# A six-block decoder on one core: stage order re-sought with a plan that counts changes of the matmul tile shape, and the top rows of the second attention turned in one transposition

## What is computed

```python
x = layernorm(x + attention0(x))      # 32 heads; low-rank q and kv, rope, causal softmax, 128 wide values
x = layernorm(x + adjacency(ctx, x))  # top-k mask of ctx Q K^T (64 wide), symmetrised
x = layernorm(x + experts(x))         # 7 routed experts (top 2) and a shared one, 256 wide
x = layernorm(x + attention1(x))      # 16 heads of 16, rope, causal softmax; see below
x = layernorm(x + bilinear(x, ctx))   # kv = ctx W_k; softmax(layernorm((x kv) kv^T))
x = layernorm(x + ffn(x))             # silu(x Wg) * (x Wu), 1024 wide, then down

# attention1
q, k = rot(q), rot(k)
scores = einsum('bthd,bshd->bhts', q, k / 4)
attn = softmax(scores + causal_mask)
ctx = einsum('bhts,bshd->bthd', attn, v)
```

## Time and profile before

| | |
|---|---|
| median of 3 runs | 703.93 us (702.81 to 706.13) |
| span of the profiled execution | 700.4 us |
| busy PE | 680.6 us (97%), 4886 matmuls |
| busy DVE, ACT, POOL | 531.1 us (76%), 494.1 us (71%), 394.8 us (56%) |
| chain that ended last | PE 77%, POOL 9%, DVE 8%, issue 3% |

### The profile page before, as it was taken

How to read it: one execution, slowest core, us unless ns; L and a number is a source line. 1 busy time by engine, 2 the same in 40 slices (tenths; PEclk the granted TensorE clock), 3 DMA queues, 4 the chain that set the end, 5 groups by cost and what they waited for, 6 DMA issues and landing times.

```text
span 700.4 us, 14717 instructions
## 1 busy us (share of the span) xinstructions
PE 680.6 (97%) x4886; PEld 574.7 (82%) x4886; DVE 531.1 (76%) x1677; ACT 494.1 (71%) x1276; POOL 394.8 (56%) x657
## 2 busy tenths in 40 slices
PE   8899999999999999999998999999989999999995
PEld 6578998888888888888886888898977787678885
DVE  2678989888697869878889776565689777866537
ACT  3789774888659784788879786646766686857631
POOL 4659732885267741698867655544791322435625
PEclk9999999999999999999999999999999999999999
DMA  8671001240341401122012002111120000101201
GB/s 293 167 229 42 17 1 40 53 122 2 109 133 32 122 1 54 46 54 61 2 49 89 1 28 63 47 46 46 46 91 3 5 2 4 48 1 46 91 1 60
DMA packets 34418, 41.06 MB, mean 59 GB/s; under 512 B 6620, under 2 KB 27238, under 8 KB 34344
## 3 DMA queue, kind: packets, MB, share of 16 engines
q1 hardware_dynamic: 33800, 39.80, 19.4%
q10 hardware_dynamic: 544, 0.33, 0.2%
HBM read 30.02 MB, written 1.05 MB: 44 GB/s over the span
## 4 chain that ended last, share of the span: by engine, by line
PE 77%; POOL 9%; DVE 8%; issue 3%; DMA 1%; SPq 1%; ACT 0%; POOLq 0%; DVEq 0%
PE bank L1184 68%; PE bank L1198 8%; POOL stat L2341 3%; POOL qT L2341 1%; PE bank L1455 1%; POOL probs L2338 1%; DMA qT<-xT_plain 1%; DVE top_tok L2238 1%; POOL probs L2341 1%; POOL w_split_lo L2341 1%; DVE g_pair_lo L1896 1%; SPq L2622 1%; DVE y L1899 1%; POOL stat L2338 1%; DVE bn L1911 1%
## 5 line engine op out<-in xcount | busy, mean ns | idle before, releaser
L2338 POOL TENSOR_SCALAR probs<-probs,soft 128x256 f32<-128x256 f32 (+1 forms) x256 | 104.5, 429 | 48.4 <-DVE soft L2031 46.7
L1686 ACT ACTIVATE probs<-probs,soft 128x256 f32<-128x256 f32 (+1 forms) x256 | 113.0, 447 | 13.5 <-DVE soft L2023 12.9
L1184 PE MATMUL bank<-xT_hi,w_split_hi 128*128 128x512 f32 x256 | 103.7, 405 | 3.5 <-POOL w_split_lo L2341 3.2
L2341 POOL TENSOR_TENSOR w_split_lo<-w_raw,w_split_hi 128x512 fp32r<-128x512 f32 (+2 forms) x57 | 72.3, 1275 | 55.1 <-ACT w_split_hi L1592 54.9
L1184 PE MATMUL bank<-xT_lo,w_split_hi 128*128 128x512 f32 x256 | 101.0, 394 | 0.0
L1184 PE MATMUL bank<-keyT,qT 128*128 128x256 f32 (+1 forms) x512 | 93.4, 330 | 0.5 <-POOL qT L2341 0.3
L2023 DVE CUSTOM_DVE_ANT_0 probs<-bank,mask 128x256 f32<-128x256 f32 (+1 forms) x256 | 78.9, 353 | 19.8 <-PE bank L1184 19.1
L1184 PEld LDWEIGHTS bank<-keyT,qT 128*128 128x128 f32 x512 | 81.8, 190 | 12.3 <-issue 2.5
L2341 POOL TENSOR_TENSOR qT<-qT,xT_plain 64x512 f32<-64x512 f32 x44 | 57.0, 1295 | 57.6 <-DMA qT<-xT_plain 55.5
L1184 PE MATMUL bank<-xT_hi,w_split_lo 128*128 128x512 f32 x192 | 75.9, 395 | 0.0
L1592 ACT ACTIVATE qT<-bank 64x512 f32<-64x512 f32 (+1 forms) x80 | 47.4, 592 | 33.1 <-PE bank L1184 30.6
(11 more groups left out here) (240 smaller groups left out, 1822.0 us busy)
## 6 DMA issues: line engine op xcount, KB each, us to landing
qT<-xT_plain SPq DMA_DIRECT2D x88, 64.0 KB, 2.0
w_raw<-in_w_nopeT SPq DMA_DIRECT2D x8, 512.0 KB, 3.6
w_raw_heads<-in_w_o SPq DMA_DIRECT2D x8, 512.0 KB, 5.1
qT<-rope_buf SPq DMA_DIRECT2D x40, 64.0 KB, 2.0
w_raw<-in_w_gateT SPq DMA_DIRECT2D x8, 256.0 KB, 2.8
w_raw<-in_w_upT SPq DMA_DIRECT2D x8, 256.0 KB, 3.3
w_raw<-in_w_downT SPq DMA_DIRECT2D x8, 256.0 KB, 3.8
w_raw<-in_L_ffn_Wup SPq DMA_DIRECT2D x7, 256.0 KB, 2.8
```

The source lines that it names most:

```text
L1184: return t.matmul(out, lhsT, rhs, start=start, stop=stop, skip_group_check=shared)
L1686: ins = s.activation(p[:, at], p[:, at], ACT.Exp, bias=st[:, 0, r:r + 1], scale=-1.0, accum_out=st[:, 1, r:r + 1])
L2338: return g_.tensor_scalar(out, in0, s1, s2, op0, op1)
L2341: return g_.tensor_tensor(out, in0, in1, op)
```

## The change

Two edits. The planner gets a cost for PE as well: a stage whose tile shape (`kind`) differs from that of the PE stage before it starts `MODE` later, a stage of the same shape gets `KEEP` on its level, and `NEAR` of PE goes from 0 to 0.15, so that a slightly later stage of the same shape can be taken. Stages get their shapes (`cols64`, `cols32`, `rows64`, `quarter`) and new estimates, and `URGENT` is a new table (some 300 numbers, of which a line stands here). Second, `top_tok` and `top_rows` are laid out so that both tiles of queries of four heads stand side by side in a tile of 128 columns, 16 of them maxima (8 high, 8 low) and the others zero; one transposition of 128x128 turns them all, ACT copies 16x128, and each of the four DMAs reads four rows of 128 instead of two of 256. POOL clears the three `top_rows` buffers once in `rows1`.

```diff
-    HOP, TABLE = 0.2, 1.3
+    HOP, TABLE, MODE = 0.2, 1.3, 0.13
+    KEEP = 222
-    NEAR = {"PE": 0.0, "ACT": 0.3, "DVE": 0.3, "POOL": 0.5, "SP": 0.3, "DMA": 0.1, "WAY": 0.0}
+    NEAR = {"PE": 0.15, "ACT": 0.3, "DVE": 0.3, "POOL": 0.5, "SP": 0.3, "DMA": 0.1, "WAY": 0.0}
...
-        ("adj_mask", 2, 1): 49, ("adj_top", 1): 241, ("adj_top", 2): 86, ("adj_top", 3): 133, "adj_top": -33,
...
+        ("adj_T", 3): 1371, ("adj_mask", 2, 0): 230, ("adj_mask", 3, 0): 336, "adj_mask": 506, "adj_sim": -546,
...
                     t = max(ready, free[engine], since)
-                    if kind and kind != table:
+                    if engine == "PE":
+                        t += self.MODE * (kind != tile)
+                    elif kind and kind != table:
                         t += self.TABLE
...
+            def stays(step):
+                engine, _, kind = self.parts[step][running[step][0]]
+                return engine == "PE" and kind == tile
+
             t, step, engine, taken = max((c for c in could if c[2] == soonest[2] and c[0] <= near),
-                                         key=lambda c: (level[c[1]], -c[0]))
+                                         key=lambda c: (level[c[1]] + self.KEEP * stays(c[1]), -c[0]))
...
-                stage(("s1", b, g, p), "PE 0.5, DVE 1.2", ("qkT", b, g), ("consts",),
+                stage(("s1", b, g, p), "PE:rows64 0.46, DVE 1.2", ("qkT", b, g), ("consts",),
...
-    top_tok = several(sb, "top_tok", 3, [P, TB, GH])
-    top_rows = several(sb, "top_rows", 3, [P, TB, 2, GH], F32R)
-    topT = several(sb, "topT", 3, [2 * GH, S], F32R)
+    top_tok = several(sb, "top_tok", 3, [P, TB * GH])
+    top_rows = several(sb, "top_rows", 3, [P, P], F32R)
+    topT = several(sb, "topT", 3, [2 * TB * GH, P], F32R)
...
+    def top_at(j, p):
+
+        first = (j * (GH // 2) + p) * TB
+        return slice(first, first + TB)
+
+    def top_part(n, c):
+        return top_rows[n][:, c * TB * GH:(c + 1) * TB * GH]
...
-                for i in range(TB):
-                    ins = transpose(out[0:2 * GH, i * P:(i + 1) * P],
-                                    plain(top_rows[top1_turns.place[b, g]][:, i, :, :]).rearrange("p c h -> p (c h)"))
-                ins.then_inc(topT_ready.sem, 1)
+                transpose(out[:, 0:P], plain(top_rows[top1_turns.place[b, g]][:, :])).then_inc(topT_ready.sem, 1)
...
-                copy(topT[top1_turns.place[b, g]][:, :], bank_of(("top_T", b, g))[0:2 * GH, 0:S]).then_inc(topT_copied.sem, 1)
+                copy(topT[top1_turns.place[b, g]][:, :], bank_of(("top_T", b, g))[0:2 * TB * GH, 0:P]).then_inc(topT_copied.sem, 1)
...
+                for t in top_rows:
+                    own(g_.memset(plain(t[:, :]), 0.0))
...
-                        q.dma_start(plain(qT1[n][row:row + 1, :, :]),
-                                    plain(topT[place][c * GH + j:(c + 1) * GH:2, :])).then_inc(top_landed_at[place], 16)
+                        first = c * TB * GH + top_at(j, 0).start
+                        q.dma_start(plain(qT1[n][row:row + 1, :, :]).rearrange("o p (i s) -> o (p i) s", i=TB),
+                                    plain(topT[place][first:first + TB * GH // 2, :])).then_inc(top_landed_at[place], 16)
```

More of the change, by code:

```diff
@@ L301, in arrange @@
     def arrange(self):
-        level, ends, starts, table = self.levels(), {}, {}, ""
+        level, ends, starts, table, tile = self.levels(), {}, {}, "", ""
         free = defaultdict(float)
@@ L440, in make_plan @@
               holds=[bank("absorb", g, left=(("w_q", g), "DVE"))])
-        stage(("w_v", g), "PE 1, ACT 0.6, DVE 0.6", ("load", g), *before,
+        stage(("w_v", g), "PE:cols64 0.8, ACT 0.6, DVE 0.6", ("load", g), *before,
               holds=[bank("vo", g, left=(("w_v", g), "DVE"))])
@@ L463, in make_plan @@
                       + [Hold("probsT", (b, g, h), By(("pv", b, g), "PE")) for h in heads], items=2)
-            stage(("pv", b, g), "PE 1.5, ACT 0.57, DVE 0.6", ("pT", b, g, 0), ("pT", b, g, 1),
+            stage(("pv", b, g), "PE:cols64 1.22, ACT 0.57, DVE 0.6", ("pT", b, g, 0), ("pT", b, g, 1),
                   holds=[bank("pv", b, g, left=(("pv", b, g), "DVE")), Hold("ctx", (b, g), By(("out", b, g), "PE"))])
-            stage(("out", b, g), "PE 1.52, DVE 0.6", ("pv", b, g), ("w_v", g), ("load", "x"), ("consts",),
+            stage(("out", b, g), "PE 1.42, DVE 0.6", ("pv", b, g), ("w_v", g), ("load", "x"), ("consts",),
                   holds=[bank("out", b, g, left=(("out", b, g), "DVE"))])
@@ L482, in make_plan @@
               holds=[bank("adj_T", b, left=(("adj_T", b), "DVE"))])
-    stage(("ctx_tok",), "PE 2.5, DVE 0.6", ("load", "xattn"), ("load", "ctx"), By(("down_T", 1), "PE"),
+    stage(("ctx_tok",), "PE:rows64 1.9, DVE 0.6", ("load", "xattn"), ("load", "ctx"), By(("down_T", 1), "PE"),
           holds=[bank("ctx_tok", left=(("ctx_tok",), "DVE"))])
-    stage(("ctx_T",), "PE 1.8, ACT 1.1", ("load", "xattn"), ("load", "ctx"), By(("down_T", 1), "PE"),
+    stage(("ctx_T",), "PE:quarter 1.75, ACT 1.1", ("load", "xattn"), ("load", "ctx"), By(("down_T", 1), "PE"),
           holds=[bank("ctx_T", h, left=(("ctx_T",), "ACT")) for h in range(NHALF)], items=2)
@@ L505, in make_plan @@
     for h in range(NHALF):
-        stage(("route_lin", h), "PE 1.45, ACT 0.6", *[("xT", "experts", b) for b in halves(h)], ("load", "router"),
+        stage(("route_lin", h), "PE:cols32 0.95, ACT 0.6", *[("xT", "experts", b) for b in halves(h)], ("load", "router"),
               holds=[bank("route_lin", h, left=(("route_lin", h), "ACT"))])
@@ L563, in make_plan @@
             stage(("top_split", b, g), "ACT 0.2, DVE 0.2", *[("s1", b, g, p) for p in range(GH // 2)])
-            stage(("top_T", b, g), "PE 0.15, ACT 0.28, SP 2.3, WAY 2", ("top_split", b, g),
+            stage(("top_T", b, g), "PE 0.15, ACT 0.25, SP 2.3, WAY 2", ("top_split", b, g),
                   holds=[bank("top_T", b, g, left=(("top_T", b, g), "ACT"))])
-            stage(("pv1", b, g), "PE 1.02, ACT 0.45", *[("st1", b, g, p) for p in range(GH // 2)], ("v1", b), *every_expert,
+            stage(("pv1", b, g), "PE:cols32 0.88, ACT 0.45", *[("st1", b, g, p) for p in range(GH // 2)], ("v1", b), *every_expert,
                   holds=[bank("pv1", b, g, left=(("pv1", b, g), "ACT")),
@@ L577, in make_plan @@
         transposed("bilinear", b, "ACT", ("bi_norm", b))
-        stage(("bi_kv", b), "PE 0.9, ACT 0.4", ("xT", "bilinear", b), ("ctx_tok",), *[By(("bi_sim", b - 2), "PE")] if b >= 2 else [],
+        stage(("bi_kv", b), "PE:cols64 0.87, ACT 0.4", ("xT", "bilinear", b), ("ctx_tok",), *[By(("bi_sim", b - 2), "PE")] if b >= 2 else [],
               holds=[bank("bi_kv", b, left=(("bi_kv", b), "ACT"))])
-        stage(("bi_sim", b), "PE 1.06", ("bi_kv", b), ("ctx_T",), holds=[bank("bi_sim", b, left=(("sim_stats", b), "DVE"))])
+        stage(("bi_sim", b), "PE:rows64 0.87", ("bi_kv", b), ("ctx_T",), holds=[bank("bi_sim", b, left=(("sim_stats", b), "DVE"))])
         stage(("sim_stats", b), "DVE 2.2, POOL 2.0", ("bi_sim", b), ("load", "attn1"),
@@ L2237, in vector_program @@
                             w.wait_ge(*left)
-                    v.reduce_max(top_tok[top1_turns.place[b, g]][:, :, 2 * p + j], two(bank_of(("s1", b, h))), AX).then_inc(top1.sem, 1)
+                    v.reduce_max(top_tok[top1_turns.place[b, g]][:, top_at(j, p)], two(bank_of(("s1", b, h))), AX).then_inc(top1.sem, 1)
             elif name == "top_split":
```

91 lines of the change are left out of this document (48 added, 43 removed), and 54 rows, old and new, of the table URGENT.

## The result

The changed kernel took 704.83 us (median of 20 runs, 703.02 to 708.0), the kernel before 702.49 us beside it (20 runs, 701.1 to 706.13): a ratio of 1.0035, 95% interval 1.0024 to 1.0046. It is a third of a per cent slower; 699.0 was forecast, and a range of 696.3 to 703.2. The forecast was 4.9 us under a kernel before at 703.93; the change came out 2.3 us over the 702.49 beside it, so the forecast is off by 7.2 us. By the bound of half a per cent this is "the same", with the whole interval above 1.

A forecast was written before the change was run, and what follows sets the result against it. The prediction took PE's own sequence as the bound (busy 680.6 of 700.4 us). Terms 2.3 + 1.8 + 0.4 + 0.9 - 0.5 gave 4.9 us less than 703.93: 699.0 us, range 696.3 to 703.2.

The forecast's parts named there:

- Term 1: PE, mostly second attention: tile shape changes fall from 183 to 160, at 0.10 us each, 2.3 us less.
- changes of shape aren't saved: Rival: the 0.10 us is only a group's end, paid elsewhere, so the shape saving is nothing: 701.3 us, chance 0.05.
- The sign that the text named: If the first attention isn't shorter by 0.3 us for its three changes of shape, the price is wrong.
- narrow transpositions were changes: Rival: the old 8-column top-row transpositions were shape changes, so 34 go, 3.4 us less: 697.9 us, chance 0.03.
- Term 2: Top rows, second attention: one transposition in place of two, 16 times at 0.11 us, 1.8 us less on PE.
- Term 3: Start: w_split_lo comes earlier, PE goes on 1.5 us sooner, w_v now runs behind: 0.4 us less.
- the clock's rival: Rival: the clock stays up at the start, so a further 1.7 us goes: 697.3 us, chance 0.17.
- Term 4: Door of second attention: v1 covers 1.5 of 1.7 us wait, new 0.6 us wait before first qkv: 0.9 us less.
- Term 5: Second attention: s1 stages in a row make PE wait for DVE's maxima, 0.5 us more, at worst 3.
- a new wait over 2 us: Sign: such a wait anywhere in the experts, whose order the prediction didn't go through, would make the forecast wrong.

The follow-up runs named there:

- e14: e13 with each extra 256-column matmul done as two 128*64 tiles side by side, adding 64 changes of shape: 724.74 us, 1.0302 of the kernel before.
- e13: e1 with one plain f32 matmul of 256 columns in 128*128 ahead of each of 32 e_gate outputs: 714.66 us, 1.0158 of the kernel before.
- e1: The kernel before with only the new layout and single transposition of the top rows, in the old order of stages: 702.13 us, 0.9982 of the kernel before.
- e15: e1 with six extra unread matmuls ahead of the first q stage and six ahead of the first qkT: 701.14 us, 0.9973 of the kernel before.
- e6: e4 with the DMAs of the second q stage moved ahead of a weight load on SP: 703.43 us, 1.0016 of the kernel before.
- e7: e4 with the second attention's row maxima taken over half of the keys only: 700.0 us, 0.9967 of the kernel before.
- e8: e1 with the second attention's row maxima taken over half of the keys only: 699.04 us, 0.9948 of the kernel before.
- e4: The changed kernel with one DVE stage, the last transposed batch's low part, moved ahead of the expert picking: 702.64 us, 0.9998 of the kernel before.
- e10: e1 with POOL's rope and clearing of the first qkv ahead of one last-block weight split: 703.42 us, 1.0014 of the kernel before.
- e2: The changed kernel with the old layout and two transpositions of the top rows, in the new order of stages: 707.39 us, 1.0053 of the kernel before.
- e5: e4 with POOL's rope of the second qkv ahead of a last-block weight split: 703.23 us, 1.0014 of the kernel before.
- e9: e4 with two POOL stages moved ahead of the last block's weight splits and six unread matmuls in PE's experts wait: 703.63 us, 1.0019 of the kernel before.
- e11: e1 with two 64-column f32 matmuls in 128*128 ahead of each of 32 e_gate outputs: 713.91 us, 1.0163 of the kernel before.
- e12: e11 with the two small matmuls as two halves of 128*64: 715.17 us, 1.0177 of the kernel before.
- e3: The changed kernel with 12 unread matmuls in PE's 3.2 us wait at the first expert: 703.28 us, 1.0004 of the kernel before.

## Why the prediction was wrong

**Term 1, changes of shape (2.3 us less): the mechanism right, the size perhaps a little small.** The ledger, with its cap of 0.13 a change, has 2.6 to 2.8 for the 23; at e14's 0.16 it would be 3.7. The rival "changes of shape aren't saved" had the price at nothing, and e14 against e13 refutes that; that the 23 fewer changes of this order reach the kernel's time is argued from the ledger and not shown by a run of its own. The sign that the text named, a first attention shorter by 0.3 us, can't be read: its last `pv` stage starts anywhere from 353.8 to 355.9 in the profiles here, old order or new. The second rival, "narrow transpositions were changes", has little for it: if they were changes, e1 would have saved 11 more of them (194 less 183), 1.1 to 1.8 us on top of the 1.8, and it gained 1.3.

**Term 2, the transposition (1.8 less): the mechanism right, 1.3 measured** in both orders. Within the noise the four DMAs of many more pieces and the copy cost about the difference or nothing.

**Term 3, the start (0.4 less) and the clock's rival: the sum's 0.4 is about what was left.** PE went on at 22.8 and the clock stayed up, as the rival had it, worth 1.9 us at that point. Over all the profiles here the first `q` stage starts at 22.6 us on average in the new order (eight) and 24.0 in the old (eight, without e15), and five of the eight are at full clock all through the first 355 us, where each of the nine of the old order has a stretch of 3.4 us at half clock in the first 52. What failed is the rival's step that such a gain reaches the end: the last `pv` stage of the first attention starts at 354.6 in the new order and 355.0 in the old (averages, with a spread of 0.6 to 0.7 each, so that the 0.4 isn't clear of it). The next stages wait for `qT`, whose swap is a DMA; e6 took that wait away, and PE then waited 1.60 us for POOL's `probs`.

**Term 4, the door (0.9 less): mis-sized.** The new wait ahead of the first `qkv` was 1.0 us and not 0.6, that for `q_rows` and `k_rows` 1.2 and not 0.2: 0.5 more than before in all, not 0.9 less. The step that failed is that POOL's end stands still while the 14 matmuls of `v1` pass. `q_rows` came 4.2 us later (512.40 before, 516.62 after). POOL reached this piece 3.0 us later, and in it there is one more split of 1.3 us. POOL before, then after:

```profile
508.65 1.29 POOL L2341 TENSOR_TENSOR w_split_lo<-w_raw,w_split_hi 128x512 fp32r<-128x512 f32 x1
509.91 1.29 POOL L2341 TENSOR_TENSOR probs<-rope_tmp,rope_tmp 128x512 f32<-128x512 f32 x1
...
512.40 0.72 POOL L2341 TENSOR_TENSOR q_rows<-probs,q_rows 128x256 fp32r<-128x256 f32 x1
```

```profile
511.62 2.54 POOL L2365 TENSOR_TENSOR w_split_lo<-w_raw,w_split_hi 128x512 fp32r<-128x512 f32 x2
514.12 1.28 POOL L2365 TENSOR_TENSOR probs<-rope_tmp,rope_tmp 128x512 f32<-128x512 f32 x1
...
516.62 0.72 POOL L2365 TENSOR_TENSOR q_rows<-probs,q_rows 128x256 fp32r<-128x256 f32 x1
```

I had read PE's order at this place and not POOL's.

**Term 5, the waits of the second attention (0.5 more): mis-sized, about 1.8 more** by the ledger, 1.4 with DVE relieved. It is about midway to the worst bound (3), and not more DVE's doing than in the old order: e7 and e8 gain alike.

**What stood outside the sum: the main step that failed.** The text said that the forecast was wrong if a new wait over 2 us stood in the experts, through whose order it didn't go. That is where it stood: 3.2 us against 1.4, with half clock behind it. e4 gives 2.6 us for undoing half of it. The order was costed where the text looked at it and put at nothing elsewhere, without a reason; the runs have 2.6 us there. The clock was a term only at the start: the wait at the door of the second attention lay in a stretch at 1.00, and I took that as evidence that waits amid steady work don't lower it. In after, e1 and e10 the clock falls behind or in them.

Added up by the ledger, for the order alone: waits took 5.3 us and the clock 1.8, the shapes gave back 2.6 and small change 0.3, which is the 4 us or so between the profiles of e1 and after (4.0 from first matmul to last); the runs have 3.7 between before and e2.

**Still open:** why the mended orders (e5, e6, e9, e10) give back what they gain. Each removed or shortened one wait, and a later wait or half clock took it: POOL's `probs` in e6, DVE's `top_tok` in e9, ACT's `qT` in e10. No run took away such a second wait too.

## What to carry over

An order of stages is a whole: a term for what is saved at each neighbour needs a pass through all new waits, since one stage put too early on PE cost a wait of 3.2 us in place of 1.4, with half clock behind it, and moving a single stage on DVE gave back 2.6, about as much as the 23 saved changes are put at. A wait of PE costs more than itself when the clock falls behind it, so price it with what the profile shows behind such waits, and try matmuls that nobody reads in it. And an experiment that prices a mode needs a control bound by the same thing.

## What the runs showed of the hardware

- Thirty-two pairs of changes from 128\*128 to two halves of 128\*64 and back cost 10.1 us (7.6 to 12.6 by the intervals), 0.32 a pair, and 0.36 in the distances of starts (e14 against e13). The way in is 0.09 to 0.10 of it (31 places in e1: 0.095); the rest isn't split between the way out and the halves themselves.
- f32 to fp32r in the same shape costs nothing (e13); the recorded starts shift by 0.2 us and shift back.
- A plain f32 matmul of 64 columns in 128\*128 takes 0.11 us for each of its two entries (e11); two halves of 128\*64 share that time (e12).
- Ahead of the last block each profile here has one to three stretches of 3.4 to 6.8 us at half clock (and one more in the last block), each near a wait of PE of 1 to 3 us, though not each such wait has one. At one place busy matmuls took it away: four profiles with a wait of 1.8 us have the stretch (e4 to e7) and the one with the wait filled hasn't (e9). In e3 and e15 too the stretch behind the filled wait is gone.
